# Weight products in halves inside the first steps, the bias product late in column tiles, and the moments of x behind the first adds of counts

## What is computed

```python
h   = relu(layernorm(x))
msg = (h[src] + edge) @ Wm.T + bm
agg = segment_sum(msg, dst) / max(deg, 1)
u   = concat(h, agg) @ Wu.T + bu
x   = x + layernorm(h + gelu(u)) * gamma + beta
h   = relu(layernorm(x))
x   = x + relu(((1 + eps) * h + segment_sum(h[src], dst)) @ W1 + b1) @ W2 + b2 + h
```

## Time and profile before

| what | value |
|---|---|
| time, median of 3 runs | 491.05 us (490.82 to 491.95) |
| the profiled execution's own time | 492.31 us |
| its span, first to last instruction | 490.5 us |
| PE busy | 473.2 us, 96% |
| DVE busy | 269.6 us, 55% |
| ACT, POOL busy | 158.1 us, 122.2 us |
| mean granted PE clock | 0.996 |
| moved by DMA | 98.92 MB |

### The profile page before, as it was taken

One profiled execution on the slowest core, in us unless ns is written; L12 is line 12 of the kernel. 1 busy time (PEld: TensorE's weight loads), 2 busy tenths in 40 slices (PEclk: granted clock), 3 DMA queues, 4 the chain that ended last, 5 costly groups with the idle time before them and its releaser, 6 DMA issues.

```text
span 490.5 us, 9290 instructions
## 1 busy us (share of the span) xinstructions
PE 473.2 (96%) x3275; PEld 277.9 (57%) x3275; DVE 269.6 (55%) x621; ACT 158.1 (32%) x291; POOL 122.2 (25%) x183
## 2 busy tenths in 40 slices
PE   4999999999999999999999999799999999999997
PEld 3445555555455446776765656699844449544442
DVE  4789878787878888877857789923100000011011
ACT  6726633332333338411037377630012122000000
POOL 4005433444343432000001112339990000000000
PEclk9999999999999999989999999999999999999999
DMA  8998999999999999988430102040140000010111
GB/s 293 383 353 294 404 386 391 390 409 403 396 385 391 403 408 409 384 328 272 169 109 23 43 23 60 0 172 1 20 152 1 0 0 1 21 43 21 44 43 38
DMA packets 31640, 98.92 MB, mean 202 GB/s; under 512 B 3592, under 2 KB 4616, under 8 KB 31594
## 3 DMA queue, kind: packets, MB, share of 16 engines
q1 hardware_dynamic: 30458, 97.27, 52.7%
q10 hardware_dynamic: 1136, 1.05, 0.7%
HBM read 95.76 MB, written 2.56 MB: 200 GB/s over the span
## 4 chain that ended last, share of the span: by engine, by line
PE 81%; DVE 10%; DMA 4%; issue 2%; SPq 1%; POOL 1%; DVEq 0%; POOLq 0%
PE ps L1354 14%; PE ps L1339 14%; PE ps L1090 10%; PE ps L1136 7%; PE ps L1189 6%; PE ps L1109 6%; PE ps L1190 5%; PE ps L1286 4%; PE ps L1098 4%; DMA X<-in_x_dram 4%; PE ps L1118 4%; PE ps L1262 3%; PE ps L1263 3%; DVE A L695 2%; DVE stats L776 1%
## 5 line engine op out<-in xcount | busy, mean ns | idle before, releaser
L421 POOL TENSOR_TENSOR aggT<-turned_sums,aggT 128x88 f32 x118 | 62.5, 529 | 88.1 <-ACT turned_sums L486 74.9
L1024 DVE TENSOR_TENSOR U<-ps,U 128x512 f32<-128x512 f32 (+1 forms) x10 | 6.9, 692 | 128.4 <-PE ps L1354 128.4
L695 DVE TENSOR_TENSOR A<-ps,A 128x220 f32 x158 | 60.7, 384 | 28.6 <-PE ps L1109 18.0
L1354 PE MATMUL ps<-W2s,hid 128*128 128x512 f32 (+1 forms) x160 | 68.8, 592 | 0.0
L1339 PE MATMUL ps<-aggT,W1s 128*128 (+1 forms) x192 | 67.3, 513 | 0.0
L1090 PE MATMUL ps<-ea,oneD 128*22 128x256 f32 x944 | 62.7, 383 | 0.0
L1339 PEld LDWEIGHTS ps<-aggT,W1s 128*128 128x128 f32 x192 | 36.4, 190 | 30.7 <-issue 30.6
L1354 PEld LDWEIGHTS ps<-W2s,hid 128*128 128x128 f32 (+1 forms) x160 | 30.0, 188 | 38.2 <-issue 38.2
L480 ACT COPY packed_sums<-ps 128x256 f32<-128x256 f32 x59 | 22.0, 372 | 91.5 <-PE ps L1090 91.5
L1090 PEld LDWEIGHTS ps<-ea,oneD 128*22 128x22 f32 x944 | 22.6, 101 | 46.5 <-issue 21.7
L1262 PE MATMUL ps<-AR,Hh 128*128 128x256 f32 (+1 forms) x160 | 44.1, 311 | 1.0 <-DVE Hl L991 1.0
(11 more groups left out here) (133 smaller groups left out, 641.7 us busy)
## 6 DMA issues: line engine op xcount, KB each, us to landing
ea<-in_edge_attr_dram SPq DMA_DIRECT2D x78, 1024.0 KB, 7.9
X<-in_x_dram SPq DMA_DIRECT2D x1, 2304.0 KB
xt<-in_x_dram SPq DMA_DIRECT2D x9, 256.0 KB, 2.8
out_dram<-U SPq DMA_DIRECT2D x9, 256.0 KB
W1s<-in_L_gnn_W_dram SPq DMA_DIRECT2D x1, 2048.0 KB, 8.8
W2s<-in_L_gnn_W_dram SPq DMA_DIRECT2D x1, 2048.0 KB, 8.4
WuN<-in_L_gnn_Wu_dram ACTq DMA_DIRECT2D x2, 512.0 KB, 4.2
WuN<-in_L_gnn_Wu_dram SPq DMA_DIRECT2D x1, 1024.0 KB, 7.0
```

The lines of the kernel that those rows point to most:

```text
L421: nc.gpsimd.tensor_tensor(cols, sums, cols, ALU.add).then_inc(early_step, 1)
L695: V.tensor_tensor(cols, ps[:, 4 + m % 2, half * KW:(half + 1) * KW].rearrange("p (h w) -> p h w", w=W), cols, ALU.add).then_inc(add_step, 1)
L1354: last = T.matmul(ps[0:rows, 6 + b % 2, :], hid[:, k, b * P:b * P + rows], W2s[:, k, :], start=k == 0, stop=k == KC - 1)
```

## The change

- Only two products of CT are made before the loop (`EAGER = 2`). Products 2 and 3 are each cut into two halves of two matmuls; the halves stand in steps 0, 1 and 2, 3.
- The bias product leaves step 1. In step 48 four matmuls of 32 columns each, in four column tiles, give partial sums; ACT copies them to `bm_parts`; in step 51 one matmul with ones adds them over partitions; DVE copies the result in step 52. `bmB` is now a column of bm in zeros, and POOL also sets `onesP`.
- DVE takes no moments before the loop. It waits for `offrow` first, and takes moments of tiles 0 to 2, 3 to 5 and 6 to 9 behind the adds of counts of steps 0, 1 and 2; `nb0` comes in step 3.
- `H0_AT` begins at step 4 (was 2). `T_AT` is 5, 6, 9, 12, 15, 21, ... (was 4, 5, 6, 9, 15, 21, ...). `QUARTERS` loses step 12 and gains step 54.
- WmN, Wu2T, bmB, `onesP` and `bm_parts` lie in the memory of Hh instead of U; ACT's first write to Hh (step 58) waits for the last product.

```diff
-    EAGER = FC - 1
-    MOMENTS = 7
+    EAGER = 2
+    MOMENTS = [(0, 3), (3, 6), (6, NT)]
...
-    H0_AT = list(range(2, 2 + NT))
-    T_AT = [4, 5, 6] + list(range(9, 9 + 6 * (NT - 3), 6))
-    QUARTERS = [n for n in range(7, FULL) if len(COUNTS[n]) == 1 or (n % 6 == 0 and 6 < n < 48)]
+    PRODUCT_AT = {k: (k - EAGER) * 2 for k in range(EAGER, FC)}
+    BIAS_PRODUCT_AT = [48, 51]
+    H0_AT = list(range(4, 4 + NT))
+    T_AT = [5, 6, 9, 12] + list(range(15, 15 + 6 * (NT - 4), 6))
+    QUARTERS = [n for n in range(7, FULL) if len(COUNTS[n]) == 1 or (n % 6 == 0 and 12 < n < 48) or n == 54]
...
+            def bias_parts_out():
+                act.wait_ge(bm_mm, 1)
+                nc.scalar.copy(bm_parts[:], ps[:, ASIDE_BANK["product", FC], :]).then_inc(bm_out, 1)
...
+                for k in PRODUCT_AT:
+                    if PRODUCT_AT[k] + 1 == n - 1:
+                        product_out(k)
+                if BIAS_PRODUCT_AT[0] == n - 1:
+                    bias_parts_out()
...
-            dve.wait_ge(x_in, 32)
-            x_moments(0, MOMENTS)
             dve.wait_ge(offs_in, 16)
...
-                if n == 0:
-                    x_moments(MOMENTS, NT)
+                if n < len(MOMENTS):
+                    if n == 0:
+                        dve.wait_ge(x_in, 32)
+                    x_moments(*MOMENTS[n])
+                if n == len(MOMENTS) - 1:
                     x_variances()
-                if n == 2:
+                if n == len(MOMENTS):
                     dve.wait_ge(rs_ready, 1)
...
+            def bias_parts():
+                pe.wait_ge(bmB_done, 3)
                 for m in range(FC):
+                    last = T.matmul(ps[m * QUAD:(m + 1) * QUAD, ASIDE_BANK["product", FC], :], bmB[:, m, :], Wu2T[:, m, :], start=True, stop=True)
+                last.then_inc(bm_mm, 1)
+
+            def bias_product():
+                pe.wait_ge(bm_out, 1)
+                T.matmul(ps[:, ASIDE_BANK["product", FC], :], onesP[:], bm_parts[:], start=True, stop=True).then_inc(ct_mm, 1)
```

More of the change, by code:

```diff
@@ L71, in gnn_kernel @@
     SMALL_AT = 16
-    assert len(ASIDE) == FC + 1 - EAGER + 2 * NT and len(QUARTERS) == FC * NT and QUARTERS[-1] < FULL and GEN_AT + 1 == U_AT[5][0]
+    assert len(ASIDE) == FC + 1 - EAGER + 2 * NT and not set(QUARTERS) & set(T_AT + BIAS_PRODUCT_AT) and len(QUARTERS) == FC * NT and QUARTERS[-1] < FULL and GEN_AT + 1 == U_AT[5][0]
     assert all(T_AT[b] + 2 <= U_AT[b][0] for b in range(NT)) and GEN_AT not in ASIDE
@@ L102, in gnn_kernel @@
     Hl, _ = place("Hl", [P, NT, D], F32R, x_at)
-    Hh, _ = place("Hh", [P, NT, D], F32R)
-    U, u_at = place("U", [P, NT, D], F32)
+    Hh, hh_at = place("Hh", [P, NT, D], F32R)
+    U, _ = place("U", [P, NT, D], F32)
     A16, a16_at = place("A16", [P, HB, AW], U16)
@@ L111, in gnn_kernel @@
     WuN, _ = place("WuN", [P, FC, 2 * D], F32, agg_at)
-    Wu2T, _ = place("Wu2T", [P, FC, D], F32, u_at + 10240)
-    WmN, _ = place("WmN", [P, FC, D], F32, u_at)
-    bmB, _ = place("bmB", [P, FC, P], F32, u_at + 8192)
+    WmN, _ = place("WmN", [P, FC, D], F32, hh_at)
+    Wu2T, _ = place("Wu2T", [P, FC, D], F32, hh_at + 8192)
+    bm_parts, _ = place("bm_parts", [P, D], F32, hh_at + 16384)
+    bmB, _ = place("bmB", [P, FC, QUAD], F32, hh_at + 18432)
+    onesP, _ = place("onesP", [P, P], F32, hh_at + 18944)
     acc, _ = place("acc", [P, NP], U16, w1_at)
@@ L400, in _ @@
             nc.gpsimd.iota(iotaP[:], [[1, 256], [0, 2]], base=0, channel_multiplier=0, allow_small_or_imprecise_dtypes=True).then_inc(consts, 1)
+            nc.gpsimd.memset(onesP[:], 1.0).then_inc(bmB_done, 1)
+            nc.gpsimd.memset(bmB[:], 0.0).then_inc(bmB_done, 1)
             pool.wait_ge(bm_in, 16)
-            nc.gpsimd.tensor_copy(bmB[:], bmC[:].rearrange("p (m a) -> p m a", a=1).broadcast_to([P, FC, P])).then_inc(bmB_done, 1)
+            pool.wait_ge(bmB_done, 2)
+            nc.gpsimd.tensor_copy(bmB[:, :, 0:1], bmC[:].rearrange("p (m a) -> p m a", a=1)).then_inc(bmB_done, 1)
             pool.wait_ge(consts, 3)
@@ L527, in _ @@
                     turned_copy(n - 1)
+                for k in PRODUCT_AT:
[3 more added lines that the diff above has]
+                    bias_parts_out()
                 if n - 1 in ASIDE:
                     kind, k = ASIDE[n - 1]
-                    if kind == "product" and k < FC:
-                        product_out(k)
-                    elif kind == "transpose":
+                    if kind == "transpose":
                         transposed_h0(k)
@@ L819, in _ @@
                         add_sums_of(n - 1, half, sum_first[half])
[L821 to L822 removed]
+                if n < len(MOMENTS):
[3 more added lines that the diff above has]
+                if n == len(MOMENTS) - 1:
                     x_variances()
[L824 removed]
+                if n == len(MOMENTS):
                     dve.wait_ge(rs_ready, 1)
                     V.scalar_tensor_tensor(nb0[:], mv[:, :, 0], -1.0, rs0[:], ALU.mult, ALU.mult).then_inc(nb_ready, 1)
[L827 to L830 removed]
+                if n - 1 == BIAS_PRODUCT_AT[1]:
+                    bias_out()
                 for b in range(NT):
@@ L1045, in _, with product @@
                 transpose_wu(n)
-            def product(k):
+            def product(k, first=0, count=FC):
                 if k < 2:
                     pe.wait_ge(wuT_done, 2 * FC - 1 + k)
-                if k == FC:
-                    pe.wait_ge(bmB_done, 1)
-                for m in range(FC):
-                    last = T.matmul(ps[:, ASIDE_BANK["product", k], :], WmN[:, m, k * P:(k + 1) * P] if k < FC else bmB[:, m, :], Wu2T[:, m, :],
-                                    start=m == 0, stop=m == FC - 1)
-                last.then_inc(ct_mm, 1)
+                for m in range(first, first + count):
+                    last = T.matmul(ps[:, ASIDE_BANK["product", k], :], WmN[:, m, k * P:(k + 1) * P], Wu2T[:, m, :], start=m == 0, stop=m == FC - 1)
+                if first + count == FC:
+                    last.then_inc(ct_mm, 1)
+            def bias_parts():
+                pe.wait_ge(bmB_done, 3)
+                for m in range(FC):
+                    last = T.matmul(ps[m * QUAD:(m + 1) * QUAD, ASIDE_BANK["product", FC], :], bmB[:, m, :], Wu2T[:, m, :], start=True, stop=True)
[3 more added lines that the diff above has]
+                T.matmul(ps[:, ASIDE_BANK["product", FC], :], onesP[:], bm_parts[:], start=True, stop=True).then_inc(ct_mm, 1)
             def transpose_indices(mine, to, ready):
@@ L1154, in aside @@
                     bank_free(ASIDE_ORDER[order - 2])
-                if kind == "product":
-                    product(k)
+                if kind == "product" and k < FC:
+                    product(k, 0, 2)
+                elif kind == "product":
+                    bias_parts()
                 elif kind == "transpose":
@@ L1204, in _ @@
                             u1(b, f)
+                for k in PRODUCT_AT:
+                    if PRODUCT_AT[k] + 1 == n:
+                        product(k, 2, 2)
+                if n == BIAS_PRODUCT_AT[1]:
+                    bias_product()
                 if n in ASIDE:
```

10 lines of the change are left out of this document (5 added, 5 removed).

## The result

The changed kernel takes **495.62 us** (494.64 to 496.27), against 491.05. The ratio is 1.0078, 95% interval 1.0058 to 1.0098, so 2.8 to 4.8 us slower; it is drawn from all executions of both kernels and is not the quotient of the two medians, which would be 1.0093. The forecast was 493.4, with 490.8 to 495.2 as its range: right in direction and short in size. The median of 495.62 lies 2.2 us above the forecast and 0.4 above the range; by the ratio the new time is 494.9 (1.0078 times 491.05), 1.5 above the forecast and inside the range.

A forecast was written before the change was run, and what follows sets the result against it. PE was taken to bound most of the span, but DVE's adds the front up to about 48 us. Front 1.2, step 12 -0.44 and late steps +1.6 gave +2.4 us: 493.4 us against 491.05, range 490.8 to 495.2.

The forecast's parts named there:

- DVE's walk, POOL's power, ACT's place in the chain: Front: offrow at 25.8, DVE's adds and moments, POOL's power at 40.85, ACT's copies, then normalization; PE's first transposes at 47.0.
- `sums(7)` +1.2: Front of PE's loop: sums(7) starts at 50.1 against 48.90, 1.2 us late.
- Step 12, -0.44: Loop step 12: transposes of 0.52 us stand in place of a quarter of 0.96, saving 0.44 us.
- Steps 48, 51 and 54, +1.6: Late steps: tiles 1.0, ones matmul 0.96 and quarter 0.96, less three gaps of 0.44, cost 1.6 us.
- They are hidden, and a later PE only gives them more time: Edge group transfers: 7.9 us from issue to landing, covered by buffers refilled three steps or more before use.
- The sum of +2.4: End of the counts: 1.2 - 0.44 + 1.6 gives +2.4 us, with everything behind shifting along.
- it lies 1.26 above the median of 491.05, which becomes 493.4: Last step: the profiled 492.31 us becomes 494.7; taking it as 1.26 above the median gives 493.4 us.
- PE's clock falls: Rival: PE idling in steps 1 and 5 lowers its clock; behind step 5 it costs 1.7 us, 495.1; chance 0.10.
- `offrow` in time: Rival: offrow lands before 23.3, DVE's walk starts 2.5 us earlier; 490.9 us, no change; chance 0.12.
- PE sets the pace in front: Rival: PE, not DVE, bounds the first steps, so removed PE work counts whole; -2.9, 488.1 us; chance 0.08.
- Normalization not late: Rival: POOL's adds or ACT's copies run quicker, transposes at 45.3, sums(7) as today; 492.2 us; chance 0.10.
- Tiles don't overlap: Rival: the bias product's column tiles in step 48 run without overlap; +2.6, 496.0 us; chance 0.03.

The follow-up runs named there:

- e1: Changed kernel with POOL's power moved behind its adds of groups 0 and 1; 490.74 us, ratio 0.9996 to the kernel before.
- e9: The changed kernel itself measured and profiled once more; 494.89 us, ratio 1.0076 to the kernel before.
- e8: Changed kernel with only the first half of each edge group 40 to 63 loaded; one execution, span 492.6 us.
- e11: Kernel before with only the first half of each edge group 40 to 63 loaded; one execution, span 490.2 us.
- e2: Changed kernel with seven tiles of moments back ahead of the wait for offrow, nb0 in step 2; 494.02 us, ratio 1.0051 to the kernel before.
- e3: Kernel before with only the change's later moments, nb0 in step 3, and its H0_AT, T_AT and QUARTERS; 495.53 us, ratio 1.0078.
- e7: e1 with bias column tiles in step 4, ones matmul in step 5, transposes moved from step 6 to 48; 495.31 us, ratio 1.0065 to kernel before.
- e10: e1 with only the bias column tiles moved, from step 48 to step 4; 491.63 us, ratio 0.9991 to the kernel before.
- e12: Changed kernel with the four bias matmuls accumulated in one column tile instead of four side by side; one execution, span 498.1 us.
- e4: Kernel before with only the bias product late (tiles in step 48, ones matmul in 51), in the change's memory; 493.03 us, ratio 1.0029.

## Why the prediction was right and where it was wrong

- **DVE's walk, POOL's power, ACT's place in the chain:** the order of waits came as forecast, and e1 shows the mechanism: take the power out from ahead of the adds and the front gains 2 us. In the first profile DVE and POOL are within 0.41 us of the forecast up to the first add of sums; behind it the second half of group 1's add takes 1.07 us, not 0.38, and the transposes start at 47.68, 0.7 late. In e9 the power starts at 40.10, 0.75 earlier than forecast, the add is as slow (1.06), and the transposes start at 46.95 (47.0).
- **`sums(7)` +1.2:** +1.92 and +1.19. The second hit is in part luck, an early walk against a slow add.
- **Step 12, -0.44:** -0.43 in both profiles. **Steps 48, 51 and 54, +1.6:** +1.32 (each cost 0.87 or 0.88, not 0.96 to 1.0; the gaps went away as said, and the copies of ACT and DVE cost nothing).
- **"They are hidden, and a later PE only gives them more time":** wrong in some profiles. Edge groups cost 0.31 us in the profile of the kernel before and 0.55 in the first of the changed one (steps 59 to 61), and some 0.4 in e9 (at 101.07), where a landing took 10.1 us; in e8 and e11 the waits at steps 59 to 61 are gone.
- **The sum of +2.4** in the profile: +3.15 in the first (492.31 to 495.46), +2.34 in the second (494.65), 2.4 between the spans of e8 and e11. It was right within 0.8; what it lacked in the first profile is the slow add and a wait for an edge group. That the second fits so well is in part luck: there a wait of 0.4 at 101 us stands against one of 0.3 in the kernel before.
- **The term that was mis-sized most is the last of the sum, "it lies 1.26 above the median of 491.05, which becomes 493.4".** The 491.05 is a median of three executions. In the sessions of the experiments the kernel before ran 67 times, between 490.26 and 494.36 us, with a median of 492.08, so its profile lies 0.23 above its median and not 1.26. The 11 executions of the changed kernel lie between 494.62 and 496.63, median 495.46. Added to 492.08, the sum of 2.4 gives 494.5: 1.0 short of that median and not 2.
- **What the rest goes with is the clock.** The record has the mean granted clock of each timed execution. In the kernel before it is 0.999 or 1.000 in 19 of the 67, with a median of 490.65 us, and 0.992 to 0.997 in 48, with a median of 492.46 (the two groups overlap). The changed kernel never had the first kind: its 11 executions are at 0.990 to 0.996. Nor had e2 (11 executions), e3 (6) and e7 (6); e1 had 3 in 12 and e10 had 6 in 12. Against the 48 the changed kernel is 3.0 us longer, against all 67 it is 3.4. Of the 14 profiles none shows such an execution: 13 have a fall near 220 us, behind the one-column matmuls, and e2, without it, has one at 32 us and a span 1.5 us shorter than its `sums(61)` asks for. Where the falls of the timed executions lie isn't recorded, so that the change's waits are the cause is not shown.
- **The rival "PE's clock falls"** was given 0.10. In one of four profiles with this front (e12) it happened, behind the very wait it named, and cost 2.7 us from the first transposes to `sums(7)` (5.81 in place of 3.14), not 1.7. The kernel before has no wait of PE over 1.15 us in these steps.
- **Rivals:** `offrow` in time, fell (the read waits, in e3 for 2.56 us). PE sets the pace in front, fell (e4: 3.6 us less PE work gave 0.57). Normalization not late, fell (PE waits 2.12 us for it in both profiles). Tiles don't overlap, fell (0.88 us side by side, 3.4 in one tile, e12).

## What to carry to other kernels

An engine that looks full may be full of cheap filling: before taking work out of it, walk what it then waits for, in every in-order list on the way (here one power ahead of the adds in POOL's list was worth 2 us), and ask what the new wait does to its clock. Moving a small piece late costs its whole price if the late steps are full; in a wait in front it was free, but the buffers and banks that it holds must be walked too. A sum made against one profile gives the difference of two profiles. Before it is carried to a median of three executions, look at how many executions that median rests on and at the granted clock of each: here the executions of the kernel before fell into two groups 1.8 us apart, one of them with a granted clock of 0.999 or more.
